# Second layer's routed experts computed on scored token-expert pairs sorted by expert, in four parts, beside a dense shared expert

## The chip, the core and the metric

The kernel is one program on one core of a Trainium2 chip. The metric is the device time of one execution in microseconds (us), lower is better. The core has a matrix engine (TensorE, PE in the rows; its weight loads stand apart as PEld), three engines that work on 128 partitions in parallel (VectorE = DVE, ScalarE = ACT, GpSimd = POOL), and a queue engine (SyncE = SP) that here only starts transfers. Each engine takes its instructions in program order; between engines only semaphores count. POOL starts the indirect transfers (one row address for each of the 128 partitions). Data lie in SBUF (128 partitions), matmul results in PSUM (eight banks of 512 fp32 columns, `ps[:, bank, :]`).

## What is computed

`x` holds 8 sequences of 512 tokens of 128 numbers. Two layers, each `x = x + s * silu(ffn)`, where `s` is a recurrence (layer 0) or a causal linear attention (layer 1), and both read the layer-normalised `x`. The change is in the feed-forward part of layer 1:

```
def _L1_ffn_ref(x, gate_w, w1, w2, w3, w1s, w2s, w3s):   # 8 experts, hidden size 128, TOP_K = 2
    scores = softmax(xt @ gate_w.T)
    top_scores, sel = top_k(scores, TOP_K)
    order = argsort(sel.reshape(-1), stable=True)
    token_idx, eid = order // TOP_K, sel.reshape(-1)[order]
    routed_in = xt[token_idx] * top_scores_sorted[:, None]
    for e in range(NUM_EXPERTS):
        xe = where(eid == e, routed_in, 0)
        h = silu(xe @ w1[e]) * (xe @ w3[e])
        out_routed += where(eid == e, h @ w2[e], 0)
    hs = silu(xt @ w1s[0]) * (xt @ w3s[0])               # the shared expert, all tokens
    out = hs @ w2s[0]
    out = out.at[token_idx].add(out_routed)
```

The score multiplies the input of an expert, not its output. All weights and results are fp32.

## The kernel before

**Layer 0.** Tokens are sorted by group of experts into 35 tiles of 128 rows with 32 indirect scatters (L394), and `late_slot(n)` runs one tile after the other for n = 0 to 34: gate and up as three fp32r products each (L838 to L840: rounded weight and rounded input, rounded weight and rest, rest and rounded), the hidden tile's turn (L868), the down product in fp32 (L858), and an indirect transfer that brings the tile's rows home to DRAM (`bring_home`, L404 on POOL). SP loads them again sequence by sequence into `xnT` (`load_y`, L329): sequences 0 to 2 after the first 16 tiles, 3 to 7 only when tile 34 is home.

**Layer 1** runs sequence after sequence, j = 0 to 7, each in 18 slots u. Slot u is half an expert: `gate_up(j, u)` makes one 512-column product of the gate or up weight of expert u // 2 with all 512 tokens, again as three fp32r products (L956 to L958). DVE multiplies the routed ones by the token's score for this expert, spread over all partitions (`scaled`, L1470; the score is 0 where the expert isn't chosen), ACT takes the silu (L654), POOL multiplies gate and up (`hidden1`, L440), and PE adds `unit_down` (L967, fp32, 512 columns) of all nine experts into one bank. So every token passes every expert. The result has features on partitions, and `turn_result` (L972) turns it back. Score rows go through DRAM: SP stores them and loads them again, spread over 128 partitions (1 MB each, two for a sequence, L338).

Between these slots lie, by numbers written out in the code, the attention of the same sequence (`scores` L913, `turn_keys` L920, `sum_state` L928, `attend` L940 and L942, masks L1434, `attended` L1449) and the preparation of the next two (gated result `gated` L1344 and L1347, statistics `stats1` L1351, `variances` L1357 to L1360, `scales` on POOL L421 and L423, `normalised` L602, turn L888, `values` with the router's columns L895, `query` L900, `key` L903, `relu` and exponentials L620 to L630, router order `ranks` L1380 to L1385, `scored` L1389 to L1394). The ranks say for each token and expert how many experts are ahead of it; rank below 2 is chosen.

## Time and profile before

| | |
|---|---|
| runs | 408.09, 412.56 and 543.4 us, median 412.56 us |
| profiled execution | 414.17 us, of which its span (first to last instruction) 412.3 us |
| mean granted TensorE clock | 0.959 of 2.4 GHz |
| busy | PE 383.7 us (93%), PEld 282.1, DVE 269.9 (65%), ACT 224.7 (54%), POOL 218.6 (53%) |

Share of PE in 40 equal slices of the span, in tenths, and the clock in tenths of full speed:

```profile
PE   7979673799999999899999999999999999999995
PEclk9868777799999999999999999999999999999999
```

Layer 0's slots begin near slice 8 (80 us), layer 1's near slice 18 (181.5 us) and run to the end. Matmuls overlap one another, so what one costs is read as the distance between two starts, not as its own duration.

### The profile page before, as it was taken

The page shows a single profiled execution, that of the slowest core. Times are in us where ns is not written, and L with a number is a line of the kernel's source. Part 1 is how long each engine was busy: PE and PEld are TensorE (multiplying, and loading weights), DVE is VectorE, ACT ScalarE, POOL GpSimd, SP SyncE. Part 2 cuts the span into 40 slices and gives each one's busy share as a digit, 9 for nine tenths or more (in the row PEclk, how much of TensorE's full clock was granted, in tenths as well). Part 3 has the DMA queues.
Part 4 walks back from the last instruction along what each step waited for, and adds up shares of the span by engine and source line. Part 5 has one row for each costly group of instructions (what it writes and reads, how often), then busy time and mean ns, then how long its engine had stood idle before and what let it go on. Part 6 is the DMA issues. An engine that isn't in the chain of part 4 may idle for free.

```text
span 412.3 us, 6279 instructions
## 1 busy us (share of the span) xinstructions
PE 383.7 (93%) x1853; PEld 282.1 (68%) x1853; DVE 269.9 (65%) x755; ACT 224.7 (54%) x447; POOL 218.6 (53%) x214
## 2 busy tenths in 40 slices
PE   7979673799999999899999999999999999999995
PEld 5674321598989888786666767667677667676772
DVE  5988942353434365527959859779689598676563
ACT  3667453454554557768756464493574664742311
POOL 4437876017653344247653936827638549268362
PEclk9868777799999999999999999999999999999999
DMA  8996311601001200006080050140410601503200
GB/s 230 243 345 255 104 52 52 172 4 36 21 25 45 80 27 19 21 33 231 2 293 16 21 212 0 51 181 1 161 72 0 232 1 29 203 0 118 115 25 26
DMA packets 26400, 38.70 MB, mean 94 GB/s; under 512 B 2640, under 2 KB 22608, under 8 KB 23936
## 3 DMA queue, kind: packets, MB, share of 16 engines
q1 hardware_dynamic: 24224, 33.87, 25.2%
q0 software_dynamic: 2144, 4.44, 3.2%
q8 instruction: 16, 0.26, 0.3%
q14 instruction: 16, 0.13, 0.1%
HBM read 29.22 MB, written 9.08 MB: 93 GB/s over the span
## 4 chain that ended last, share of the span: by engine, by line
PE 72%; DVE 10%; ACT 9%; another core or an unknown queue 3%; issue 3%; DMA 1%; POOL 1%; SPq 0%; POOLq 0%; DVEq 0%; ACTq 0%
PE ps L967 10%; PE ps L858 7%; PE ps L958 6%; PE ps L956 6%; PE ps L957 6%; PE ps L779 5%; PE ps L838 4%; PE ps L840 4%; PE ps L839 4%; PE ps L868 4%; PE ps L942 3%; PE ps L895 2%; DVE score L1394 2%; DVE pr L1391 2%
## 5 line engine op out<-in xcount | busy, mean ns | idle before, releaser
L440 POOL TENSOR_TENSOR gu<-gu 128x512 f32<-128x512 f32 x64 | 84.0, 1317 | 86.6 <-DVE gu L1470 81.4
L956 PE MATMUL ps<-xc_round,w_round 128*128 128x512 f32 x144 | 82.8, 575 | 0.6 <-DVE gu L1458 0.5
L654 ACT ACTIVATE gu<-gu 128x512 f32<-128x512 f32 x64 | 40.3, 630 | 75.3 <-DVE gu L1470 75.2
L967 PE MATMUL ps<-gu,w2s 128*128 128x512 f32 x144 | 73.4, 593 | 0.5 <-POOL gu L440 0.5
L404 POOL DMA_INDIRECT home_y<-sorted_sb,home x35 | 34.1, 974 | 70.6 <-ACT sorted_sb L581 46.5
L958 PE MATMUL ps<-xc_round,w_rest 128*128 128x512 f32 x144 | 56.9, 395 | 0.0
L957 PE MATMUL ps<-xc_rest,w_round 128*128 128x512 f32 x144 | 56.5, 393 | 0.0
L1470 DVE TENSOR_TENSOR gu<-ps,w_raw 128x512 f32<-128x512 f32 x64 | 43.8, 687 | 19.0 <-PE ps L958 18.4
L1320 DVE TENSOR_TENSOR sx_rest<-ps,sx_round 128x128 fp32r<-128x128 f32 x35 | 10.2, 291 | 63.4 <-ACT sx_round L567 54.1
L838 PE MATMUL ps<-w_round,sx_round 128*128 x70 | 35.0, 501 | 10.3 <-issue 6.2
L576 ACT COPY h0T<-ps 128x512 f32<-128x512 f32 x35 | 20.6, 587 | 43.5 <-PE ps L868 42.1
L394 POOL DMA_INDIRECT sorted_rows<-sorted_sb,slot x32 | 33.4, 1044 | 15.8 <-issue 9.5
L858 PEld LDWEIGHTS ps<-w0d,h0T 128*128 128x128 f32 x280 | 36.5, 191 | 3.4 <-issue 0.4
L956 PEld LDWEIGHTS ps<-xc_round,w_round 128*128 128x128 f32 x144 | 27.3, 190 | 15.8 <-issue 12.1
L957 PEld LDWEIGHTS ps<-xc_rest,w_round 128*128 128x128 f32 x144 | 27.4, 190 | 14.5 <-issue 12.9
L858 PE MATMUL ps<-w0d,h0T 128*128 x280 | 36.9, 275 | 0.0
L967 PEld LDWEIGHTS ps<-gu,w2s 128*128 128x128 f32 x144 | 26.7, 188 | 8.2 <-POOL gu L440 1.5
L1330 DVE SCALAR_TENSOR_TENSOR h<-sg,sorted_sb,ps 128x256 f32<-128x256 f32 x70 | 30.2, 473 | 3.1 <-PE ps L868 2.6
L958 PEld LDWEIGHTS ps<-xc_round,w_rest 128*128 128x128 f32 x144 | 27.0, 188 | 6.1
L1470 DVE TENSOR_TENSOR gu<-ps,w0d 128x512 f32<-128x512 f32 x32 | 21.7, 688 | 12.4 <-PE ps L958 12.3
L779 PE MATMUL ps<-xnT,a0w 128*128 128x512 f32 x48 | 29.3, 761 | 0.0
L840 PE MATMUL ps<-w_rest,sx_round 128*128 x70 | 28.5, 408 | 0.0
(202 smaller groups left out, 768.5 us busy)
## 6 DMA issues: line engine op xcount, KB each, us to landing
w_raw<-score_rows SPq DMA_DIRECT2D x8, 1024.0 KB, 6.7
sorted_sb<-score_rows SPq DMA_DIRECT2D x4, 1024.0 KB
w0d<-score_rows SPq DMA_DIRECT2D x4, 1024.0 KB, 6.9
sorted_rows<-zero_rows SPq DMA_DIRECT2D x1, 2358.0 KB, 16.5
xa<-in_x SPq DMA_DIRECT2D x8, 256.0 KB, 5.1
w_raw<-in_gate_up SPq DMA_DIRECT2D x1, 2048.0 KB, 13.7
xnT<-home_y SPq DMA_DIRECT2D x8, 256.0 KB, 6.9
out_x<-xa SPq DMA_DIRECT2D x7, 256.0 KB, 2.4
```

The source lines that it names most:

```text
L404: pool.indirect_dma_start(home_y, bass.IndirectOffsetOnAxis(ap=home[:, n:n + 1], axis=0), sorted_sb[:, n, 0:P], None).then_inc(y_home[0 if ...
L440: pool.tensor_tensor(gu[:, e % RING, 1, :], gu[:, e % RING, 0, :], gu[:, e % RING, 1, :], ALU.mult).then_inc(s["m_h"], 1)
L654: nc.scalar.activation(gu[:, e % RING, 0, :], gu[:, e % RING, 0, :], ACT.Silu).then_inc(s["m_sg"], 1)
L779: last = pe.matmul(ps[:, 3 * par + i, :], a0w[:, i * P:(i + 1) * P], xnT[:, q * SEQ:(q + 1) * SEQ], start=True, stop=True)
L838: pe.matmul(bank, sx_round[:, par, :], w0_round[:, c], start=True, stop=False)
L840: return pe.matmul(bank, sx_round[:, par, :], w0_rest[:, c], start=False, stop=True)
L858: last = pe.matmul(ps[:, bank, 0:P], h0T[:, par, c * P:(c + 1) * P], w0d[:, bass.ds(g + c * P, P)], start=(c == 0), stop=(c == HC - 1))
L956: pe.matmul(bank, w13_round[:, c], xc_round[par][:, :], start=True, stop=False)
L957: pe.matmul(bank, w13_round[:, c], xc_rest[par][:, :], start=False, stop=False)
L958: pe.matmul(bank, w13_rest[:, c], xc_round[par][:, :], start=False, stop=True).then_inc(s["m_gu"], 1)
L967: pe.matmul(ps[:, 3, :], w2s[:, w * P:(w + 1) * P], gu[:, e % RING, 1, :], start=(e == 0), stop=(e == E1)).then_inc(s["m_y"], 1)
L1470: nc.vector.tensor_tensor(gu[:, e % RING, part, :], ps[:, BANKS[u % RING], :], spread[j % 2][(e - 1) // (E1 // 2)][:, c:c + SEQ], ALU.mult ...
```

## The change

Layer 1 no longer runs by sequence. `MAIN` is a list of 41 places b = 0 to 40: 6 empty ones, 6 quads of part 0, 6 of part 1, the shared expert of sequences 0 and 1, 6 quads of part 2, 6 of part 3, the shared expert of sequences 2 to 7, 3 empty ones. A part is two sequences: 1024 tokens, 2048 pairs of token and chosen expert, sorted by expert. Each expert's pairs are rounded up to whole tiles of 128, so a part has room for 16 + 7 = 23 tiles, and all 23 are computed; a quad is four of them (three in a part's last). Attention of sequence k is at places 3k, 3k + 1 and 3k + 2.

For a part, DVE ranks and counts (place `ROUTE_AT` = 3, 6, 15 for parts 1 to 3), PE sums the counts over partitions (`place2`), DVE works out the address of each pair, multiplies the normalised rows by their two scores and works out each tile's expert (next place). POOL scatters the rows to DRAM, eight indirect transfers for a sequence; SP loads the part's 23 tiles; after the quads it stores the results, and POOL gathers them, again eight for a sequence. A quad takes plain fp32 matmuls, weights chosen by registers loaded from `expert`. The shared expert stays dense, in fp32 too. The sum over pairs is made on DVE (`summed`). The normalised `xn` now lives in the scatter's source, the first three sequences are prepared in layer 0's slots (`GY_AT`, `TURN_AT`), the ReLU of the feature map moves from ACT to DVE, the products of gate and up from POOL to DVE, and the splitting of the layer-1 weights, the score rows' way through DRAM and the turn of the result fall away.

```diff
-T_GY = (23, 27)
-T_TURN = 27
+PART2 = ((0, 1), (2, 3), (4, 5), (6, 7))
+TILES2 = tuple(TOPK1 * TPS * len(p) + E1 - 1 for p in PART2)
+QUAD = 4
+GY_AT = (20, 23, 27)
+TURN_AT = (24, 27, 33)
+MAIN = (6 * [None] + [("q", 0, i) for i in range(QUADS2[0])] + [("q", 1, i) for i in range(QUADS2[1])]
+        + [("s", k, 0) for k in (0, 1)] + [("q", 2, i) for i in range(QUADS2[2])] + [("q", 3, i) for i in range(QUADS2[3])]
+        + [("s", k, 0) for k in range(2, SEQS)] + 3 * [None])
+ATT_AT = tuple(3 * k for k in range(SEQS))
+GATED_AT = (None, None, None, 1, 2, 3, 8, 9)
+TURNED_AT = (None, None, None, 2, 4, 5, 12, 14)
+LOGITS_AT = (None, None, None, 3, 5, 6, 13, 15)
+ROUTE_AT = (None, 3, 6, 15)
...
+            scatter_pairs(0)
+            scales(3)
+            scatter_pairs(1)
+            scales(4)
+            scales(5)
+            scatter_pairs(2)
+            scatter_pairs(3)
+            scatter_pairs(4)
+            scales(6)
+            scatter_pairs(5)
+            scales(7)
+            gather_pairs(0)
+            gather_pairs(1)
+            scatter_pairs(6)
+            scatter_pairs(7)
+            for k in range(2, SEQS):
+                gather_pairs(k)
...
+            def gather_pairs(k):
+                p = part2_of(k)
+                pool.wait_ge(pairs_stored[p], 32)
+                wait(pool, "c_z", k - GABS + 1)
+                for r in range(TOPK1):
+                    for t in range(TPS):
+                        pool.indirect_dma_start(
+                            gab[k % GABS][:, r, t, :], None, pairs_y[p],
...
+            def unit_gate(m):
+                kind, k, _ = UNITS[m]
+                wait(pe, "m_h", m)
+                if kind == "q":
+                    q = QUAD_UNITS.index(UNITS[m])
+                    pe.wait_ge(s["q_xT"], q + 1)
+                    for t in range(tiles_in(UNITS[m])):
+                        w = pe.snap(at_w13[t], min_val=0, max_val=W13 - 3 * P)
...
+                        last = pe.matmul(ps[:, GATE + t // 2, o:o + 2 * P].rearrange("p (a c) -> p a c", c=P),
...
+            for b, unit in enumerate(MAIN):
+                before = MAIN[b - 1] if b > 0 else None
+                after = MAIN[b + 1] if b + 1 < len(MAIN) else None
+                if unit:
+                    unit_gate(unit_no(unit))
+                if after and after[0] == "q":
+                    experts_of(at_w13, after, 0)
+                for k in range(SEQS):
+                    if b == ATT_AT[k] + 2:
+                        z_free()
+                        sum_state(k)
+                        z_read[0] = ("c_state_out", k + 1)
+                if before:
+                    unit_down(unit_no(before))
+                if unit and unit[0] == "q":
+                    experts_of(at_w2, unit, 1)
+                if after and after[0] == "q":
+                    turn_pairs(QUAD_UNITS.index(after))
+                for k in range(SEQS):
+                    if b == ATT_AT[k] and k > 0:
+                        query(k)
+                        key(k)
+                        z_free()
+                        values(k)
...
+            def rows_of(k):
+                dve.wait_ge(s["c_turned"], k + 1)
+                by = [score2[:, r, TPS * k:TPS * (k + 1)].unsqueeze(2).broadcast_to([P, TPS, P]) for r in range(TOPK1)]
+                link(nc.vector.tensor_tensor(rsrc[k][:, :, 1, :], rsrc[k][:, :, 0, :], by[1], ALU.mult))
+                nc.vector.tensor_tensor(rsrc[k][:, :, 0, :], rsrc[k][:, :, 0, :], by[0], ALU.mult).then_inc(s["c_rows"], 1)
...
+                for p in range(1, PARTS2):
+                    if b == ROUTE_AT[p] + 1:
+                        slots_of_pairs(p)
+                        scored(p)
+                        for k in PART2[p]:
+                            rows_of(k)
+                        experts_of_tiles(p)
```

What TensorE runs in a place. Of before, nine rows from a sequence's slots 4 to 6: two halves of a routed expert (three fp32r rows each, L956 to L958) between two downs (L967) and the state (L928); `m_free` is DVE's scaling, `m_h` POOL's product.

```order
L967 MATMUL ps<-gu,w2s 128x512 [waits m_h]
L956 MATMUL ps<-xc0_round,w13_round 128x512 [waits m_free]
L957 MATMUL ps<-xc0_rest,w13_round 128x512
L958 MATMUL ps<-xc0_round,w13_rest 128x512
L956 MATMUL ps<-xc0_round,w13_round 128x512 [waits m_free]
L957 MATMUL ps<-xc0_rest,w13_round 128x512
L958 MATMUL ps<-xc0_round,w13_rest 128x512
L967 MATMUL ps<-gu,w2s 128x512 [waits m_free,m_gf]
L928 MATMUL ps<-vo,key_rows 128x129 [waits c_keys_out]
```

Of the change, the piece from one place (b = 12) on, behind its gate matmuls: registers with the experts (`TENSOR_LOAD`), the three downs of the quad before (L1029, a weight address in an `ISA` row each), four turns of the next quad's rows (L989), query (L933, waits for the attention result of the sequence before, `c_s1`), key, and the turn of this quad's hidden tiles (L1014), which waits for DVE (`m_h`).

```order
L982 TENSOR_LOAD expert [waits expert_ready]
L1028 ISA [waits q_hT,q_y]
L1029 MATMUL ps<-w2s,hT 128x128
...
L982 TENSOR_LOAD expert [waits expert_ready]
L989 MATMUL ps<-cst,sorted_sb 128x128 [waits q_xT,pairs_in1_0]
L989 MATMUL ps<-cst,sorted_sb 128x128 x3
L933 MATMUL ps<-xnT,a1w 128x512 [waits c_s1,c_xT]
L936 MATMUL ps<-xnT,a1w 128x512
L940 MATMUL ps<-vg_w,xnT 128x128 [waits c_state_out]
L940 MATMUL ps<-vg_w,xnT 128x128 x3
L1014 MATMUL ps<-cst,hq 128x128 [waits q_hT,m_h]
L1014 MATMUL ps<-cst,hq 128x128 x3
```

The three fp32r rows of an expert half over 512 tokens have become four 256-column fp32 rows (L1001) for a quad, and one place holds one unit with what lies around it.

On DVE, the router's work of one sequence in before: nine rows, from one scaling to another. The scalings (L1470) that TensorE's banks wait for stand between all of it.

```order
L1470 TENSOR_TENSOR gu<-ps,sorted_sb 128x512
L1434 TENSOR_TENSOR at<-ps,cst 128x256
L1434 TENSOR_TENSOR at<-ps,cst 128x128
L1470 TENSOR_TENSOR gu<-ps,sorted_sb 128x512
L1389 TENSOR_REDUCE rs<-e1 128x4
L1390 RECIPROCAL rs<-rs 128x4
L1391 TENSOR_TENSOR pr<-e1,rs 128x32
L1394 SCALAR_TENSOR_TENSOR score<-rank,pr 128x4x8
L1470 TENSOR_TENSOR gu<-ps,sorted_sb 128x512
```

Of the change, the end of the same for part 2 (place b = 7, then b = 8): the last rows of a run of 30 between two products of gate and up (L1572). Twelve for the addresses (L1446 to L1459) and seven for the scores (L1478 to L1484) stand right ahead of these.

```order
L1489 TENSOR_TENSOR rows3456<-rows3456,score2 128x4x128
L1490 TENSOR_TENSOR rows3456<-rows3456,score2 128x4x128
L1489 TENSOR_TENSOR rows3456<-rows3456,score2 128x4x128
L1490 TENSOR_TENSOR rows3456<-rows3456,score2 128x4x128
L1463 TENSOR_TENSOR past2<-cst,ends2 1x168
L1466 TENSOR_TENSOR past2<-past2,step2 1x168
L1468 TENSOR_REDUCE expert_f<-past2 1x24
L1469 CAST expert<-expert_f 1x24
L1466 TENSOR_TENSOR past2<-past2,step2 1x168
L1468 TENSOR_REDUCE expert_f<-past2 1x24
L1469 CAST expert<-expert_f 1x24
L1572 TENSOR_TENSOR hq<-sgq,ps 128x512
```

The product of place 8 is the last row, behind the whole of the part's routing.

On POOL, the last rows of the change (sequences 4 to 7; `pairs_y2` holds the results of part 2, and `pairs_stored3` says that part 3's are in DRAM). In before POOL ends with products L440 and one sum L445.

```order
L487 DMA w0d<-pairs_y2,slot2 128x128 [waits c_z,pairs_stored2]
L487 DMA w0d<-pairs_y2,slot2 128x128 x7
L487 DMA w0d<-pairs_y2,slot2 128x128 [waits c_z,pairs_stored2]
L487 DMA w0d<-pairs_y2,slot2 128x128 x7
L487 DMA sorted_sb<-pairs_y3,slot2 128x128 [waits c_z,pairs_stored3]
L487 DMA sorted_sb<-pairs_y3,slot2 128x128 x7
L487 DMA sorted_sb<-pairs_y3,slot2 128x128 [waits c_z,pairs_stored3]
L487 DMA sorted_sb<-pairs_y3,slot2 128x128 x7
```

The last sixteen gathers stand behind the store of the last quads.

## Rows read from the trace of the kernel before

**Rows 1.** Windows: us, busy of PE, PEld, DVE, ACT, POOL, clock, DMA share, GB/s.

```profile
181.50:209.70 28.20, 27.05 (x138) 20.19 (x139) 19.83 (x52) 20.65 (x36) 18.51 (x16) 1.00 0.32 115
294.40:322.60 28.20, 28.01 (x125) 19.65 (x124) 22.65 (x54) 16.03 (x28) 16.64 (x14) 1.00 0.23 85
```

**Rows 2.** Groups by line: engine, tile, shape, count, busy us, mean ns, idle before.

```profile
L956 PE MATMUL ps<-xc_round,w_round 128*128 128x512 f32 x144 | 82.8, 575 | 0.6 <-DVE gu L1458 0.5
L967 PE MATMUL ps<-gu,w2s 128*128 128x512 f32 x144 | 73.4, 593 | 0.5 <-POOL gu L440 0.5
```

**Rows 3.** Timeline of PE in a sequence: start, us, line, tile, count.

```profile
301.17 1.02 PE L967 MATMUL ps<-gu,w2s 128*128 128x512 f32 x2
...
302.26 0.40 PE L957 MATMUL ps<-xc_rest,w_round 128*128 128x512 f32 x1
302.49 0.39 PE L958 MATMUL ps<-xc_round,w_rest 128*128 128x512 f32 x1
...
310.48 0.60 PE L972 MATMUL ps<-cst,gf 128*128 128x128 f32 x4
```

**Rows 4.** Timeline of POOL: indirect scatters and transfers home.

```profile
31.09 0.96 POOL L394 DMA_INDIRECT sorted_rows<-sorted_sb,slot  x1 [0.30 <-issue]
32.35 0.95 POOL L394 DMA_INDIRECT sorted_rows<-sorted_sb,slot  x1 [0.30 <-issue]
...
46.31 2.02 POOL L394 DMA_INDIRECT sorted_rows<-sorted_sb,slot  x1 [0.30 <-issue]
...
129.44 0.96 POOL L404 DMA_INDIRECT home_y<-sorted_sb,home  x1 [1.88 <-ACT sorted_sb L581]
...
177.44 1.04 POOL L421 TENSOR_TENSOR rstd<-var,minus_half 128x4 f32<-128x4 f32 x1
...
187.74 0.96 POOL L404 DMA_INDIRECT home_y<-sorted_sb,home  x1 [0.30 <-issue]
```

**Rows 5.** Timeline of SP's queue: the first loads of what came home.

```profile
131.72 1.46 SPq L329 DMA_DIRECT2D xnT<-home_y  x3
```

**Rows 6.** Page, part 6: transfers, KB each, median us from issue to landing.

```profile
xnT<-home_y SPq DMA_DIRECT2D x8, 256.0 KB, 6.9
out_x<-xa SPq DMA_DIRECT2D x7, 256.0 KB, 2.4
```

**Rows 7.** Timeline of DVE.

```profile
147.85 0.69 DVE L1344 TENSOR_TENSOR gy<-gy,sT 128x512 f32<-128x512 f32 x1
148.58 0.69 DVE L1347 SCALAR_TENSOR_TENSOR xa<-gy,xa 128x512 f32<-128x512 f32 x1
149.30 0.87 DVE L1351 BATCH_NORM_STATS2 st<-xa 128x6 f32<-128x128 f32 x4
...
176.03 0.22 DVE L1394 SCALAR_TENSOR_TENSOR score<-rank,pr 128x32 f32<-128x32 f32 x1
...
302.14 0.42 DVE L1380 TENSOR_TENSOR ahead<-lg 128x256 f32<-128x256 f32 x1
```

**Rows 8.** Groups of DVE, shapes apart.

```profile
L1449 DVE SCALAR_TENSOR_TENSOR s<-ps,den,bo 128x128 f32<-128x128 f32 x32 | 9.6, 341 | 0.0
L1237 DVE TENSOR_TENSOR past<-cst,steps 1x286 f32<-1x286 f32 x1 | 0.4, 437 | 0.0
```

**Rows 9.** Timeline of ACT: exponential, change of table, silu.

```profile
302.07 1.04 ACT L630 ACTIVATE tg<-tg 128x1024 f32<-128x1024 f32 x1
303.13 1.28 ACT L654 ACT_TABLE_LOAD   x1
304.42 0.63 ACT L654 ACTIVATE gu<-gu 128x512 f32<-128x512 f32 x1
```

**Rows 10.** Windows around TensorE's wait at the start of layer 0's slots.

```profile
64.00:68.00 4.00, 1.45 (x4) 0.38 (x2) 0.00 (x0) 2.15 (x4) 3.08 (x4) 0.97 0.20 67
68.00:72.00 4.00, 0.37 (x1) 0.38 (x2) 0.72 (x4) 1.15 (x3) 2.40 (x3) 0.50 0.15 50
```

More of the change, by code:

```diff
@@ L368, in _ @@
+            load_pairs(3)
+            store_pairs(2)
+            store_pairs(3)
+            for j in range(2, SEQS):
+                store_out(j)
+            sp.wait_ge(o_stored, 16 * SEQS)
         @block.gpsimd
@@ new lines, in logits, with place2, query @@
+                last.then_inc(s["c_logits"], 1)
+            def place2(p, bank):
+                n = TPS * len(PART2[p])
+                pe.wait_ge(s["counted2"], p + 1)
+                pe.matmul(ps[:, bank, 0:E1], lower, cum2[:, :, n - 1], start=True, stop=True)
+                pe.matmul(ps[:, bank, E1:2 * E1], ones, cum2[:, :, n - 1], start=True, stop=True).then_inc(s["placed2"], 1)
+            def query(k):
+                pe.wait_ge(s["c_xT"], k + 1)
+                wait(pe, "c_s1", k)
+                pe.matmul(ps[:, BX, :], a1w[:, 0:P], xnT_of(k), start=True, stop=True).then_inc(s["c_q"], 1)
@@ L1089, in _, with z_free @@
-            unit_down(SEQS - 1, E1 - 1)
-            unit_down(SEQS - 1, E1)
-            for i in range(2):
-                pe.wait_ge(s["m_gf"], SEQS + i)
-                turn_result(SEQS - 1, slice(2 * i, 2 * i + 2), (4, 6)[i])
+            pe.wait_ge(s["f_xr"], SORTED)
+            values(0)
+            pe.wait_ge(s["f_y"], SORTED - 1)
+            key(0)
+            pe.wait_ge(s["f_y"], SORTED)
+            pe.wait_ge(s["f_h"], SORTED)
+            z_read = [("c_vo", 1)]
+            def z_free():
+                pe.wait_ge(s[z_read[0][0]], z_read[0][1])
@@ new lines, in attended, with unit_hidden @@
+                last.then_inc(s["c_s1"], 1)
+            def unit_hidden(m):
+                kind, k, _ = UNITS[m]
+                n = tiles_in(UNITS[m])
+                dve.wait_ge(s["m_sg"], m + 1)
+                if kind == "q":
+                    ups = ps[:, GATE:GATE + 2, :].rearrange("p b c -> p (b c)").rearrange("p (t c) -> p t c", c=2 * P)[:, 0:n, P:2 * P]
+                else:
+                    ups = ps[:, GATE + 1, :].rearrange("p (t c) -> p t c", c=P)
+                quads = sum(u[0] == "q" for u in UNITS[:m])
+                wait(dve, "q_hturned", quads)
+                if m > 0 and UNITS[m - 1][0] == "s":
+                    dve.wait_ge(s["m_down"], m)
+                nc.vector.tensor_tensor(hq[:, 0:n, :], sgq[:, 0:n, :], ups, ALU.mult).then_inc(s["m_h"], 1)
```

1102 lines of the change are left out of this document (537 added, 565 removed).

## Prediction

> **What bounds the kernel now.** First the windows, one for each sequence of layer 1 [rows 1]: PE is busy 28.01 of 28.2 us, DVE 22.65, POOL 16.64, ACT 16.03, at a clock of 1.00. The sequences follow each other at this distance to the end, so in layer 1 (181.5 to 412.3 us, 230.8 us) TensorE is the bound and no other engine waits for anything but it. What it does there, the groups say [rows 2]: 144 triples that begin with L956, and 144 halves (72 matmuls) of L967. Their price is the distance between starts in the timeline [rows 3]: fp32r with 512 columns 0.23 us (302.26 to 302.49), a triple 0.69; the two halves of the fp32 down from 301.17 to 302.03 (one such step before 302.26), 0.86. Four turns cost about 0.44 (0.60 with the overlap). I take 0.21 us for an fp32 matmul of 128 columns and 0.43 for 256, a quarter and a half of 0.86.
>
> **What TensorE saves.** Of a sequence's 28.2 us, 18 triples take 12.4, nine downs 7.7, the result's turn 0.44; 7.6 stay for attention and preparation. Removed are 16 triples (11.0), 8 downs (6.9) and the turn: 18.4. The shared expert goes from 2 x 0.69 + 0.86 to three times 0.86, 0.3 more. Added are 11.5 tiles a sequence (23 for two): a turn 0.11, gate and up 0.43, a turn of the hidden tile 0.11, down 0.21, so 0.86 a tile or 3.45 a quad, 9.9 a sequence. TensorE saves 18.4 - 0.3 - 9.9 = 8.2 us a sequence, 65 in all, and needs some 165 of the 230.8. If it stayed the bound, the kernel would take 347 us. It doesn't: everything it now works on passes DVE, POOL and DRAM first, with few tiles ahead. I walk through these.
>
> **The opening, to the end of place 6.** Until here layer 0 is as before, its added work (one sequence more prepared, ranks of 8 tiles) hidden under slots of 2.8 us; the last tile goes home at about 186 instead of 187.74 [rows 4], since three triples no longer stand ahead of its down. From there:
> - POOL: a scatter comes every 1.26 us (31.09 to 32.35), eight for a sequence, 10.1 us, so sequence 0 ends at 197. Scales: 1.04 + 0.2 = 1.3. Sequence 1: 198.6 to 208.7. What POOL sends lands 1.3 us after it (transfer at 129.44 to 130.4, loads at 131.72 [rows 4, 5]); a load of 512 KB by the 6.9 us in a queue of several and the 2.4 of a single one of 256 KB [rows 6] I put at 3.5. First pairs at 213.5.
> - DVE, which is later still. Sequence 3 can only be loaded at 188, is gated and normalised by 200.3, turned at 201.3. TensorE has waited 4 us then, and goes at half clock, as in the row of 0.50 after a wait [rows 10]. Query, key and values, 2.6 us at full clock, take it to 206.5; values out 0.7, router columns 0.6: 207.9.
> - Ranks for 8 tiles: a linked 512-column operation starts every 0.73 us (147.85 to 148.58 [rows 7]), three are 2.2; five short ones of 0.22 and a gap of 0.04 (176.03) make 1.3: 3.5 us, to 211.6. Behind them on DVE stand two features (1.2), and gating and statistics of sequence 5 (1.44 + 1.5, by 0.87 for the first of three steps), to 215.7, then masks 1.2.
> - The routing block: 19 short operations 4.9, four row products 2.9, seven for the tiles' experts 2.2 (168 elements on one partition: between 0.22 and the 0.44 of 286 [rows 8]). 10.0 us, to 227. Then `attended`, four of 0.34 [rows 8] and three short, 1.7: 228.6. Only then may the query of place 6 start (`c_s1`), although the first quad's gate is done at 221.
> - Place 6: again a wait of 6 us ahead, so 4.7 us for query, key, values; out and router columns 1.5; ranks 3.5, and `place2` waits for them: 238.5.
>
> So the first 52 us hold about 22 us of TensorE's work.
>
> **Places 7 to 23.** With attention in every third place a place has 3.45 + 7.6/3 = 6.0 us of TensorE's work (5.8 where no sequence is prepared). ACT needs less: 4 copies or silus of 0.6 and, once in three places, 1.04 + 2 x 1.28 for exponential and tables [rows 9] and two ReLUs, some 4.3 a place; it costs the place after an exponential 0.5. 17 x 5.9 = 100.3. Added: the ranks of part 3 in place 15, waited for like those above, 4.6; the routing blocks of parts 2 and 3 in places 7 and 16. The product of the next quad (L1572) stands behind the block, the hidden turn behind that: masks end about where the place ends, so the turn of places 8 and 17 comes at 10.0 + 0.7 + 0.4 = 11.1 instead of 5.6: 5.5 us each, 11. For half clock after these three waits [rows 10] I add 5. Place 23 ends at 238.5 + 100.3 + 4.6 + 11 + 5 = 359.4.
>
> **Places 24 to 31**, quads alone. Gate 1.71; 0.2 until ACT sees it, silu 0.6, product 0.69, 0.1, turn 0.44 make 3.75, and the copies of the turned rows behind the result's copy 3.9, against 3.45 of PE: 8 x 3.9 = 31.2, to 390.6.
>
> **The tail.** The last results are copied out 3.1 us into place 32, their store of 704 KB takes 4 (one of 256 KB 2.4 [rows 6]). Only now do the gathers of sequences 6 and 7 start, 16 on POOL. No gather stands in the trace: the nearest row is a scatter, 1.26 with the gap; its bounds are 0.95 (no gap) and 2.32 (the row at 46.31 and the gap). I take 1.26, as it too writes 128 row addresses: 20.2, bounds 15 and 37. Landing 1.5, two sums, silu and two products 3.6, store 2.4, end 0.8. Sum 35.6 us, of which TensorE's last six shared experts (6 x 2.6) hide 15 but shorten nothing. Span 426 us. The profiled execution of before has 414.17 for a span of 412.3, and its median is 412.56, so I put the time at **426 us**, 3% over before.
>
> What hides the rest: the zeroing of the pairs' buffers (6.3 MB) delays the first tiles home, but their rows are first wanted 16 tiles on; POOL's scatters for parts 1 to 3 end 20 us and more ahead of their quads; the splitting of weights (POOL) and score rows (SP) were hidden before and give nothing.
>
> **A rule against the change.** The rows show a clock of 1.00 in layer 1 before, and 0.50 after TensorE had stood still [rows 1, 10]. The Trainium skill, "TensorE: Matmul & The Clock Gate", section "HAM oscillation — how this bites in real kernels", says that waits for transfers between bursts of matmuls send the clock back to half and that each burst pays again. By it the places after the waits are dear; if the clock stayed full, the same sum would be 4 + 5 us less, about 415.
>
> **Rivals.**
> - *The walk, slower* (426; own range 421 to 441): chance 0.56, of which 0.14 for its upper part: DVE holds up POOL. The scatter at 46.31 took 2.02 instead of 0.96 us while DVE worked on SBUF [rows 4]; if every second transfer on the path (32 of them) and the registers' loads on PE (48, not seen in before as a gap) cost that much, 15 us more, 441. The Trainium skill, "GPSIMD Engine Reference", section "1. Specifications", says that POOL shares its SBUF interfaces with VectorE and meets two-input instructions there; that row agrees.
> - *DVE's blocks are shorter, within 2%* (about 412): full clock (9 less) and short operations at 0.2 instead of 0.26 (3 us over three blocks), or landing and loads faster by 2. Chance 0.30.
> - *POOL alone sets the opening, faster* (about 392): if DVE's work in places 3 to 6 fits under POOL's chain, the first gate is at 217 and place 6 ends at 223 rather than 238.5, and if the two later blocks fit in their places too (5.5 each, and clock 5), 426 - 15.5 - 11 - 5 = 394. It decides when a block takes under 5 us. For it: before, DVE's share was below TensorE's. Against: these operations are chained one by one, and the product stands behind them. Chance 0.14.
> - *It computes no less than before.* 92 tiles for 64 tiles' worth of pairs are fixed by the room for rounding; this is in the sum.
>
> **Numbers.** About 2% is what a measurement here can tell from no change. Faster by more than 2% (under 404) 0.14, within 2% (404 to 421) 0.30, slower 0.56. The range that leaves 2 in 10 out reaches from 401 (half of the third rival) to 441: the likeliest case's own range begins at 421.
>
> **What would show it.** PE idle ahead of query L933 in place 6 and ahead of the hidden turn L1014 in places 8 and 17, 4 to 6 us each, released by DVE; clock near 0.5 right after; quads alone every 3.9 us; the last sixteen gathers 1.26 us apart with PE idle beside them. I am wrong if PE in the 17 mixed places is busy over 90%, if a gather costs far from 1.26, or if the block is under 7 us.

## The result, and the profile after

The changed kernel took **524.33 us** (median of 3, 520.13 to 527.39) beside 412.56 before: a ratio of **1.277, 95% interval 1.250 to 1.304**. The forecast was 426 us, range 401 to 441. The direction was right, and the size was not: 3% was forecast, 28% came.

Much of that turned out to depend on the chip. On another chip the same kernel took **448.75 us** beside 398.83 before, **1.129 (1.120 to 1.137)**. So there are two misses: about 37 us in the kernel's own work (448.75 beside 412, see below), and 75 us more on the first chip. In what follows "first chip" is that of the first result, and "a quiet chip" is one where the kernel before takes 396 to 402 us. (On the first chip one execution of before took 543.4 us; no trace shows why.)

Page of after, parts 1, 3 and 4: busy us, share and instructions of each engine; two DMA queues; the chain that ended last.

```profile
PE 371.2 (71%) x1965; PEld 298.8 (57%) x1965; DVE 239.5 (46%) x735; ACT 221.8 (42%) x439; POOL 229.3 (44%) x244
...
q1 hardware_dynamic: 51600, 35.31, 23.1%
q0 software_dynamic: 6240, 12.84, 8.1%
...
PE 42%; another core or an unknown queue 17%; ACT 12%; DVE 12%; issue 8%; POOL 5%; DMA 2%; SPq 1%; POOLq 0%; DVEq 0%; ACTq 0%
```

No engine is the bound: 71% of PE, 46% of DVE. A quarter of the chain (17% and 8%) is on no engine at all. The windows that answer [rows 1], and two more (us, busy of PE, PEld, DVE, ACT, POOL, clock, DMA share, GB/s):

```profile
181.50:209.70 28.20, 19.20 (x119) 16.20 (x118) 15.65 (x48) 14.28 (x29) 21.56 (x12) 0.94 0.14 44
294.40:322.60 28.20, 21.43 (x132) 18.33 (x130) 9.91 (x28) 15.70 (x29) 11.73 (x13) 0.94 0.37 105
380.00:420.00 40.00, 13.38 (x68) 10.93 (x67) 8.11 (x13) 7.27 (x11) 23.00 (x24) 0.70 0.22 62
420.00:460.00 40.00, 37.30 (x239) 31.86 (x238) 13.21 (x30) 24.12 (x41) 4.48 (x5) 1.00 0.32 89
```

Where before had 28.01 of 28.2 us of PE, after has 21.43; from 380 to 420 us it is 13.38 of 40, with POOL the busiest engine. In the 40 us behind that POOL is nearly silent and PE is back at 37.30. That contrast is the main clue. Timeline of after in the bad stretch (start, us, instruction, idle time before it and its releaser):

```profile
392.91 0.95 POOL L487 DMA_INDIRECT sorted_sb<-pairs_y,slot  x1 [0.31 <-issue]
393.78 0.59 ACT L684 COPY xT<-ps 128x512 f32<-128x512 f32 x1 [9.29 <-remote]
...
394.61 3.47 PE L1001 MATMUL ps<-w13s,xT 128*128 x8 [8.74 <-issue]
...
402.88 0.56 DVE L1544 TENSOR_TENSOR at<-ps,mask 128x384 f32<-128x384 f32 x1 [12.60 <-issue]
...
412.67 0.56 DVE L1544 TENSOR_TENSOR at<-ps,mask 128x384 f32<-128x384 f32 x1 [9.24 <-remote]
...
414.78 0.37 ACT L674 COPY key_rows<-ps 128x256 f32<-128x256 f32 x1 [19.89 <-remote]
```

Each of these ACT and DVE instructions waits for a result of TensorE. The matmuls that they wait for are recorded long before: the last of them, the turn of the keys (L954), at 385.49. The profile names no instruction that ends these waits ("remote", "issue"). Beside them POOL issues indirect transfers every 1.26 us, the last at 409.20. I call such a wait a **hold**. On the quiet chip (a_again, below) the same instructions stand like this, and no ACT, DVE or PE instruction behind 110 us has an unexplained wait over 1.8 us:

```profile
347.56 0.58 ACT L684 COPY xT<-ps 128x512 f32<-128x512 f32 x1
349.75 0.63 ACT L710 ACTIVATE zf<-zf 128x512 f32<-128x512 f32 x1 [1.61 <-DVE zf L1581]
350.28 0.35 ACT L674 COPY key_rows<-ps 128x256 f32<-128x256 f32 x1
```

### The profile page after: what moved, and what is told of

Its sections match the earlier page's. It is cut to its first block, busy times and chain, and to the rows that moved or that the text cites. A ratio compares the mean times of both kernels' runs of the same rounds, so it can differ in the third digit from the quotient of the medians.

```text
span 525.6 us, 6617 instructions
## 1 busy us (share of the span) xinstructions
PE 371.2 (71%) x1965; PEld 298.8 (57%) x1965; DVE 239.5 (46%) x735; ACT 221.8 (42%) x439; POOL 229.3 (44%) x244
## 4 chain that ended last, share of the span: by engine, by line
PE 42%; another core or an unknown queue 17%; ACT 12%; DVE 12%; issue 8%; POOL 5%; DMA 2%; SPq 1%; POOLq 0%; DVEq 0%; ACTq 0%
PE ps L1001 6%; PE ps L884 5%; PE ps L805 4%; POOL sorted_sb L487 3%; PE ps L864 3%; PE ps L894 2%; PE ps L866 2%; PE ps L865 2%; PE ps L1029 2%; POOL e L468 2%; PE ps L920 2%; ACT sorted_sb L536 1%; PE ps L1007 1%; ACT sgq L694 1%
## 5 line engine op out<-in xcount | busy, mean ns | idle before, releaser
L477 POOL DMA_INDIRECT pairs_x<-rows,slot x40 | 40.6, 1014 | 64.5 <-DVE rows L1490 53.0
L1001 PE MATMUL ps<-w13s,xT 128*128 x184 | 53.2, 440 | 18.8 <-ACT xT L684 9.7
L1572 DVE TENSOR_TENSOR hq<-sgq,ps 128x512 f32<-128x512 f32 (+1 forms) x32 | 21.4, 670 | 88.4 <-ACT sgq L694 63.0
L487 POOL DMA_INDIRECT w0d<-pairs_y,slot x32 | 30.4, 951 | 66.6 <-DMA pairs_y<-xs_even 57.5
L1001 PEld LDWEIGHTS ps<-w13s,xT 128*128 128x128 f32 x184 | 39.2, 225 | 26.3 <-issue 20.6
L487 POOL DMA_INDIRECT sorted_sb<-pairs_y,slot x32 | 32.6, 1017 | 29.6 <-DVE zf L1581 20.2
L1029 PEld LDWEIGHTS ps<-w2s,hT 128*128 128x128 f32 x184 | 26.2, 210 | 9.9 <-issue 8.9
L1029 PE MATMUL ps<-w2s,hT 128*128 x184 | 27.2, 294 | 6.0 <-ACT hT L699 4.0
L865 PE MATMUL ps<-w_round,sx_rest 128*128 x70 | 29.1, 416 | 0.0
L612 ACT ACTIVATE sg<-ps 128x512 f32<-128x512 f32 x35 | 21.0, 599 | 17.8 <-PE ps L866 11.3
L1014 PE MATMUL ps<-cst,hq 128*128 128x128 f32 x92 | 16.7, 308 | 13.7 <-DVE hq L1572 12.3
```

Source lines behind the costliest of these rows:

```text
L477: pool.indirect_dma_start(pairs_x[p], bass.IndirectOffsetOnAxis(ap=slot2[:, r, TPS * k + t:TPS * k + t + 1], axis=0), rsrc[k][:, t, r, :], ...
L487: pool.indirect_dma_start(gab[k % GABS][:, r, t, :], None, pairs_y[p], bass.IndirectOffsetOnAxis(ap=slot2[:, r, TPS * k + t:TPS * k + t + ...
L865: pe.matmul(bank, sx_rest[:, par, :], w0_round[:, c], start=False, stop=False)
L1001: last = pe.matmul(ps[:, GATE + t // 2, o:o + 2 * P].rearrange("p (a c) -> p a c", c=P), xT[:, q % 2, t * P:(t + 1) * P], w13s[:, bass.ds( ...
L1029: last = pe.matmul(ps[:, DOWN, t * P:(t + 1) * P], hT[:, t * P:(t + 1) * P], w2s[:, bass.ds(w, P)], start=True, stop=True)
```

## Experiments

### The holds by themselves

A small program (not the model) sets stretches one after another: TensorE and ScalarE hand a bank to and fro 28 times, or TensorE runs 450 matmuls in one go, beside different work of POOL and SP.

```diff
+SECTIONS = (("pa", None), ("pa", "scatter"), ("pa", "gather"), ("pa", "pool"), ("pa", "plain"),
+            ("mm", None), ("mm", "scatter"), ("mm", "gather"), ("da", None), ("da", "scatter"), ("da", "gather"), ...)
+for t in range(STEPS):                       # "pa", on PE: wait for ACT's copy t, then
+    for c in range(4): pe.matmul(ps[:, t % 2, c * P:(c + 1) * P], cst[:, 0:P], xa[:, c, :], ...)
```

(Shortened: "pa" is the to and fro of TensorE and ScalarE, "mm" the 450 matmuls, "da" VectorE with ScalarE; the second word is what runs beside it.)

> Not the model: a small program of 13 stretches that times the disputed cost by itself; its output is a copy of x. In a stretch TensorE and ScalarE hand a PSUM bank to and fro 28 times (four 128x128 fp32 matmuls, one copy), or VectorE and ScalarE do, or TensorE runs 450 matmuls in one go, and beside it stands nothing, or 36 scatters, 36 gathers, POOL products, or plain transfers of SP's queue. The profile of the changed kernel shows instructions that wait for a TensorE result and go on 2 to 20 us after its last recorded matmul, always while POOL issues indirect transfers 1.26 us apart. Theory (indirect transfers hold TensorE's results up): the to and fro takes about 28 x 1.7 = 48 us alone, beside POOL products and beside plain transfers, and 10 to 40 us more beside 36 gathers or scatters (45 us of them); the 450 matmuls lengthen by a like amount only if TensorE itself is held. VectorE with ScalarE is not lengthened. Rival (the stalls come of TensorE's register loads or of its instruction stream and the transfers only stand beside them by chance): gathers change nothing in the stretches without register loads, under 2 us each.

First copy to last: 74.3 us alone (48 were expected), 74.3 beside POOL products, 74.3 beside plain transfers, but 101.2 beside 36 scatters and 103.6 beside 36 gathers. The 450 matmuls took 102 us alone, 141 beside scatters, 135 beside gathers (POOL's transfers began at 566.73 and 707.66, the next stretch at 842.80). VectorE with ScalarE: 30.0 alone, 33.8 and 33.9 beside transfers, with no hold. With four register loads ahead of each step it was 87.7 alone and 107.0 beside gathers. ScalarE's copies beside the scatters, which ran from 99.72 to 145.14:

```profile
109.99 0.59 ACT L136 COPY cop<-ps 128x512 f32<-128x512 f32 x1 [2.17 <-issue]
112.75 0.59 ACT L136 COPY cop<-ps 128x512 f32<-128x512 f32 x1 [2.17 <-PE ps L160]
116.80 0.59 ACT L136 COPY cop<-ps 128x512 f32<-128x512 f32 x1 [3.47 <-PE ps L160]
125.27 0.59 ACT L136 COPY cop<-ps 128x512 f32<-128x512 f32 x1 [7.88 <-remote]
140.73 0.59 ACT L136 COPY cop<-ps 128x512 f32<-128x512 f32 x1 [14.87 <-remote]
150.57 0.59 ACT L136 COPY cop<-ps 128x512 f32<-128x512 f32 x1 [9.26 <-remote]
153.33 0.59 ACT L136 COPY cop<-ps 128x512 f32<-128x512 f32 x1 [2.17 <-PE ps L160]
```

The to and fro keeps its pace beside the first dozen transfers, is then held for 8, 15 and 9 us, and is free again 5 us after the last. In the 450 matmuls nothing waits for a result, and there TensorE's own starts are drawn apart (each matmul leaves two rows; scatters from 566.73):

```profile
610.47 0.37 PE L164 MATMUL ps<-cst,xa 128*128 128x128 f32 x1 [2.43 <-issue]
613.27 0.37 PE L164 MATMUL ps<-cst,xa 128*128 128x128 f32 x1 [2.43 <-issue]
616.78 0.37 PE L164 MATMUL ps<-cst,xa 128*128 128x128 f32 x1 [3.14 <-issue]
617.49 89.81 PE L164 MATMUL ps<-cst,xa 128*128 128x128 f32 x787 [0.34 <-issue]
```

From 576.7 to 617.5 it starts 30 of the 900 rows, up to 3.5 us apart, and then at once one every 0.11 us, as alone. So the holds are TensorE's, matmuls as well as what waits for them; they come beside indirect transfers in either direction, and they need nothing else of this kernel. The rival falls as far as it says register loads or chance: without register loads all four stretches beside such transfers are held. What the transfers act on isn't shown. One more rival is untested: every execution listed here has a granted clock on record, so each was recorded by the profiler, and TensorE leaves by far the most rows (900 in 102 us, as many weight loads, and VectorE with ScalarE only 56 in 30); whether TensorE is also held when nothing is recorded is open.

The same program then went on with other forms of the transfers: twelve, spaced, in bursts, fewer rows, each waited for, plain ones from POOL.

> The small program again (TensorE and ScalarE to and fro, 28 times, 77 us alone, 2.75 us each), now with other forms of the transfers beside it: 36 gathers back to back; 12 of them; 36 each followed by two POOL products (about 2.6 us apart) or by one (about 1.9 us); bursts of six with about 8 us of products between; 36 with 32 of the 128 rows; 36 that each wait for the landing of the one before; 36 plain ones issued by POOL; and 450 matmuls in one go beside 36 spaced ones. Theory A (POOL's transfers are issued faster than something behind them takes them, and TensorE is held while the backlog stands; in the first small program the holds began 13 to 14 us after the first of 36 in three stretches of three): 12 gathers cost under 2 us, spaced ones and bursts cost under 3 us each, back to back 25 to 30 us; those that wait for landing nothing. Theory B (each gather takes TensorE some 0.8 us wherever it stands): 12 cost about 10 us, the spaced ones 25 to 30 us like the others. The quarter rows tell whether rows or instructions count: under 3 us if rows.

There all nine stretches of the to and fro, "36 back to back" among them, were 74.3 us. The kernel before took 397.93 us on that chip, for 407.61 on the chip of the first small program. That made the chip itself a suspect:

> The small program with the eight forms of transfers beside TensorE and ScalarE, and two more stretches of 450 matmuls in one go, alone and beside 36 gathers back to back. On the chip of the first small program 36 transfers back to back cost TensorE 27 to 29 us in the to and fro; on the chip of the second nothing at all (74.3 us in each form). Theory (a property of the chip on which it runs, not of the program): it comes out as one of the two, all or nothing, and together with the kernel before on the same chip: holds where that takes 406 us and more, none where it takes 398 to 400. If there are holds: twelve gathers and those that wait for landing cost under 2 us, 36 back to back 25 to 30. Rival (the first program's scatters left something behind): no holds on either kind of chip, since this program has no scatter.

Again 74.3 us for each form, and 450 matmuls beside 36 gathers took 100.7 us for 102.6 alone:

```profile
776.61 102.62 PE L169 MATMUL ps<-cst,xa 128*128 128x128 f32 x900 [0.16 <-issue]
879.64 100.74 PE L169 MATMUL ps<-cst,xa 128*128 128x128 f32 x900 [0.41 <-DVEq L187]
```

The program without a scatter doesn't explain it either: m5_spacing has 36 scatters in a stretch of its own.

> The small program with two more forms: scatters, and gathers of which every eighth is waited for until it has landed. Theory (holds belong to the chip): with before at 397 to 400 us no stretch is over 75 us. On a chip with holds (before over 405): 36 back to back cost 25 to 30 us, as 36 scatters do; with a wait for landing after each eight, or 2.6 us apart, under 3 us (theory A, a backlog), or 15 us and more (theory B, each transfer).

74.3 us in all ten, the scatters' included, and m4_spacing and m6_spacing (the same forms once more) gave the same. Holds were seen on the first chip and on that of m1_side_by_side (which may be the same); none on three others, in five runs of the small program. Beside those five the kernel before took 397.9 to 399.7 us (medians; the last two share most of its executions), on the first two 412.6 and 407.6. The forms were thus never measured where there are holds; whether it is a property of the chip or of something that ran there at that time isn't settled either.

### The holds in the kernel

> The changed kernel with all 128 indirect transfers of the second layer (64 scatters, 64 gathers) replaced by plain ones of the same bytes on SP's queue, so the rows are not sorted and the result is another; all other work stands. Theory (indirect transfers hold up TensorE's results, beside POOL's own 1.26 us each): no wait for a TensorE result over 2 us that goes on after its last matmul is left behind 215 us, the second layer loses 17 to 25 per cent of the span and the time is about 400 to 430. Rival (only POOL's own time on the path goes, 20 us in the opening and 20 in the tail; the stalls of 5 to 20 us stay): 475 to 490.

```diff
-                        pool.indirect_dma_start(pairs_x[p], ..slot2.., rsrc[k][:, t, r, :], None)
+                sp.dma_start(px_t[p][:, 8 * (k % 2):8 * (k % 2) + 8, :], rsrc[k].rearrange("p t r d -> p (t r) d"))
-                        pool.indirect_dma_start(gab[k % GABS][:, r, t, :], None, pairs_y[p], ..slot2..)
+                sp.dma_start(gab[k % GABS].rearrange("p r t d -> p (r t) d"), py_t[p][:, 0:TOPK1 * TPS, :])
```

(Shortened; the rows go unsorted, one plain transfer for eight indirect ones.) 453.45 us beside 407.61: 1.116 (1.105 to 1.127). The kernel before scattered from 405.6 to 423.2 us on this chip, so each ratio found there (this one and those of a_more_gathers and a_exp_on_act) is on record as unclear; the 87 us to a_exp_on_act's 540.54 on the same chip are clear without it. It ran on a chip with holds; its last is at 114.08 us, beside the homes of layer 0's tiles, which are still indirect:

```profile
114.08 0.58 ACT L633 COPY h0T<-ps 128x512 f32<-128x512 f32 x1 [8.57 <-remote]
```

Nothing is held behind it, which is what the theory said of the trace. The time lies between the theory's range (400 to 430) and the rival's (475 to 490), 23 us over the one and 22 under the other: the theory's range left out the kernel's own 37 us, and the gate of place 6 comes at 248.5 us, 11 later than in nearly the same form on a quiet chip (a_plain_exp, below, 237.5), with the holds of layer 0 left in.

> The changed kernel with 24 more gathers on POOL behind those of sequence 3 (about 410 to 440 us), where POOL is idle and places run in 3.9 to 6 us each now; their rows go to a place nobody reads. Theory (indirect transfers hold up TensorE's results): the stretch gets stalls of 3 to 10 us and the time grows by 10 to 25 us. Rival (stalls are not tied to POOL's transfers): POOL ends them before part 2 is stored, nothing waits, under 3 us.

```diff
+            for i in range(3):
+                for t in range(2 * TPS):
+                    pool.indirect_dma_start(rows3456[:, i, t // 2, t % 2, :], None, pairs_y[0], ..slot2[:, 0, t]..)
```

559.06 us, 1.374 (1.362 to 1.385) on the chip of a_plain_all. The changed kernel itself has no run on this chip, so the cost of 24 transfers that nobody waits for, 30 us of POOL's time, is read twice: 19 us over a_exp_on_act (540.54, this chip) and 35 over the first result (524.33). From the gate of place 6 to that of place 32, where they lie, it is 269.4 us for 240.9 and 235.8: 28 and 34 more, beyond the 10 to 25 expected. ScalarE in the stretch:

```profile
420.02 0.37 ACT L681 COPY key_rows<-ps 128x256 f32<-128x256 f32 x1 [25.55 <-remote]
441.72 0.60 ACT L701 ACTIVATE sgq<-ps 128x512 f32<-128x512 f32 x1 [21.33 <-remote]
```

And the changed kernel on a quiet chip:

> The changed kernel as it stands, once more, on the chip of the small program beside it. Theory (TensorE is held beside POOL's transfers on some chips only): with holds 520 to 535 and 1.28 to 1.31 of before; without them the time is that of the work itself: the same kernel without indirect transfers, 440 to 450, and 5 to 15 us for the tail's gathers and for POOL's queue, so about 450 to 460 or 1.13 to 1.15 of before, and no hold over 2 us in the trace. Rival (the second small program only missed them, the real kernel always has them): 520 to 540 on either chip.

448.75 us, as expected without holds. Its stages against after's, by the starts of the gates L1001 and L1007: the gate of place 6 comes at 236.8 for 249.4; from there to the gate of place 24 it is 136.5 us for 189.7, places 24 to 31 take 32.2 for 46.0, the rest 40.4 for 40.4. All of it lies where POOL's transfers run beside TensorE's work.

> The changed kernel with its 64 scatters as they are and only the 64 gathers of the second layer replaced by plain transfers on SP's queue (the result is another). By the traces of the changed kernel the holds of TensorE behind 250 us that lie beside gathers sum to about 50 us (326 to 338, 386 to 415, 458 to 476) and the tail pays 16 gathers, 20 us, less what plain ones take. Theory (both kinds of transfer hold TensorE alike): 524 to about 470, and 450 is reached only when the scatters go as well, 15 to 25 us. Rival (only scatters hold it, gathers merely wait): 505 to 510.

440.08 us, 1.108 (1.100 to 1.117), on a quiet chip. It can't speak on holds there. Against a_again (1.129) it gives the gathers' own price without holds, 8 us by the ratios; 7.0 of it show in the tail (33.4 us for 40.4 from the gate of place 32 to the end). The scatters that it keeps cost nothing that can be measured (a_plain_exp without them, on the same chip, takes 443.78).

> The changed kernel, POOL's wait for the zeroing put late as in a_zero_late (1.107 of before without holds), and POOL waits for the landing of each sequence's eight scatters or gathers before the next. On a chip without holds: 1 to 2 us for each of 16 waits, nearly all off the path, so 1.11 to 1.12 of before. On a chip with holds, where the changed kernel takes 1.28 to 1.31: by theory A (a backlog behind the transfers) about 1.15, by theory B 1.26 and more.

448.59 us, 1.125 (1.117 to 1.134), on a quiet chip. Beside a_zero_late, which it contains, the sixteen waits cost 7 us, a little more than I put (1.11 to 1.12); the question it was made for stays open.

### The kernel's own 37 us

POOL's power for the exponentials of part 0 takes 10.58 us where 128x4 take 1.04 [rows 4], and I had not costed it.

```profile
169.49 10.58 POOL L468 TENSOR_TENSOR e<-euler,lg 128x64 f32<-128x64 f32 x1
```

> The changed kernel with the exponentials of part 0 made by ScalarE's Exp behind slot 30 in place of POOL's power (10.58 us at 182.7 us). Theory (the power delays the last tiles' way home and the scores of part 0, and with them the whole opening, about 204 us for 186): 10 to 15 us less, 524 to about 511. Rival (the opening is set by VectorE's chain, the power is hidden): under 4 us.

```diff
-                if n == LG_AT:
-                    powers(0)
+                if n == LG_AT + 1:
+                    router_exp(0)          # on ScalarE
```

540.54 us, 1.316 (1.298 to 1.335), not faster. Its trace has a hold of 16.78 us at 64.86, in the scatters of layer 0 that it shares with before, so the comparison said little. Twice more, without holds:

> The changed kernel with part 0's exponentials by ScalarE in place of POOL's power of 10.58 us, beside the changed kernel on the same chip. The theory of the power (it holds up the last tiles' way home and VectorE's scores): 8 to 12 us under the changed kernel. Rival, which the two runs without indirect transfers speak for (1.116 of before with the power, 1.115 without): VectorE's routing chain ahead of it ends no earlier, under 3 us.

> The changed kernel without indirect transfers in the second layer (plain ones of the same bytes on SP's queue, rows unsorted, so another result), and with the exponentials of part 0 by ScalarE instead of POOL's power of 10.58 us. Against the same kernel with the power (450 to 453 us). Theory (the power holds the way home of the last tiles and VectorE's scores, and so the opening): 8 to 12 us less, about 442. Rival (VectorE's routing chain between slots 30 and 35 sets the opening alone): under 3 us less.

1.124 (1.118 to 1.130) beside 1.129 for a_again on the same chip, and 1.115 (1.108 to 1.123) beside 1.116 for a_plain_all on another. Neither has the 8 to 12 us of the theory, so the rival holds: the power is hidden. VectorE waits 0.86 us for it (at 191.90 in a_plain_all's trace), and the homes that pile up behind it are sent 1.3 us apart until the last tile is computed anyway. The power is dear and costs nothing here.

What does cost is the row of slots. From the silu of slot 20 to that of slot 34 it is 46.5 us before and 60.9 in a_again. POOL, ACT and PE of a_again:

```profile
120.17 0.96 POOL L454 DMA_INDIRECT home_y<-sorted_sb,home  x1 [0.30 <-ACT sorted_sb L621]
...
126.30 0.63 ACT L636 ACTIVATE gy<-xnT 128x512 f32<-128x512 f32 x1 [3.61 <-DMA xnT<-home_y]
...
140.15 0.66 PE L914 MATMUL ps<-cst,tg 128*128 128x128 f32 x4 [1.75 <-ACT tg L648]
145.07 1.04 PE L920 MATMUL ps<-vg_w,xnT 128*128 128x8 f32 x8 [1.43 <-ACT xnT L654]
...
171.49 0.39 PE L927 MATMUL ps<-cum,cst 128*128 128x8 f32 x2 [1.83 <-DVE cum L1438]
```

A prepared sequence takes 0.66 + 1.04 us of PE and makes it wait 1.75 and 1.43 us, 4.9 together; there are now three of them and one totals step. The first row is the tail of a backlog: POOL waits for the zeroing before its first tile goes home.

> The changed kernel; POOL waits for the zeroing of the pairs' buffers (6.3 MB on SP's queue from 75 to about 90 us) only ahead of the first scatter of pairs instead of ahead of the first tile's way home. In the changed kernel the homes then run back to back until 124 us, the silu of sequence 0 waits 3.6 us for its rows at 126.3, and slot 20 takes 7.0 us instead of 2.8. Theory (this backlog stretches the slots): 3 to 5 us less than the changed kernel, 1.129 to about 1.118 of before on a chip without holds. Rival (the slots behind take it up): under 1 us.

```diff
-            pool.wait_ge(s["zeroed2"], 16 * PARTS2)
             for n in range(SORTED):
...
+            pool.wait_ge(s["zeroed2"], 16 * PARTS2)
             scatter_pairs(0)
```

443.12 us, **1.107 (1.100 to 1.114)**, some 8 us less than a_again by the ratios where 3 to 5 were expected, the fastest form found with the right sorting; it is still 10.7% over before. The silu of sequence 0 now follows without a wait:

```profile
119.64 0.27 ACT L621 COPY sorted_sb<-ps 128x128 f32<-128x128 f32 x1
119.80 0.65 ACT L636 ACTIVATE gy<-xnT 128x512 f32<-128x512 f32 x1
```

Slot 20 takes 3.3 us instead of 7.0, and slots 20 to 34 54.1 instead of 60.9. The remaining 7.6 us over before would be paid by two more prepared sequences of 4.9, less what is hidden; that share was read from the rows, not tried.

> The changed kernel; of the routing blocks of parts 2 and 3 on VectorE (9.2 us in one piece) the scores, the row products and the tiles' experts (about 6 us) stand behind the hidden product of the next place instead of ahead of it. In the changed kernel TensorE's hidden turn waits 3.5 us at place 8 and 4.3 at place 17 for that product. Theory (the place of the block costs what the forecast says, 5.5 us each less what is hidden): both waits go, 5 to 8 us less, 1.129 to about 1.112 of before on a chip without holds. Rival (the block moves the wait to the attention behind it, query of places 9 and 18): under 2 us less.

```diff
+                for p in range(2, PARTS2):
+                    if b == ROUTE_AT[p] + 2:      # behind unit_hidden of that place
+                        scored(p); rows_of(k) for its sequences; experts_of_tiles(p)
```

1.123 (1.119 to 1.126), 2 us less by the ratios, which can't be told from nothing: the rival's outcome (under 2). The wait ahead of the hidden turn of place 8 is gone, and a longer one stands ahead of the query of place 9. a_again:

```profile
265.24 0.98 PE L1014 MATMUL ps<-cst,hq 128*128 128x128 f32 x4 [3.52 <-DVE hq L1572]
```

and a_block_split:

```profile
269.42 2.04 PE L933 MATMUL ps<-xnT,a1w 128*128 128x512 f32 x2 [5.34 <-DVE sT L1556]
```

At the other block it is the same: 4.29 us ahead of the hidden turn of place 17 become 3.44 ahead of the query of place 18. Where VectorE's block of 9 us stands only chooses who waits.

## Why the prediction was wrong, and where it was right

The fair comparison for the sum is a_again: the sum was made on a trace that had holds of its own beside layer 0's scatters, and before is 13.7 us shorter on the quiet chip, so it says 412 there, and 448.75 was measured. (That all 13.7 us lie ahead of layer 1 is taken, not shown: no trace of before from a quiet chip is kept.) Windows of a_again, cut at the last tile's result, the query of place 6, the gate of place 24 and the shared expert behind place 31:

```profile
189.70:239.60 49.90, 32.06 (x131) 25.62 (x129) 29.19 (x99) 20.65 (x36) 26.70 (x29) 0.62 0.29 86
239.60:373.30 133.70, 110.73 (x671) 93.02 (x670) 72.01 (x194) 74.02 (x122) 75.14 (x79) 0.92 0.35 98
373.30:405.50 32.20, 29.45 (x181) 24.59 (x180) 6.54 (x13) 17.10 (x31) 14.03 (x15) 1.00 0.35 98
405.50:445.90 40.40, 18.05 (x80) 11.01 (x78) 20.26 (x30) 8.32 (x14) 19.32 (x19) 0.84 0.33 88
```

- **"Until here layer 0 is as before, its added work hidden under slots of 2.8 us": failed**, the largest step within the kernel. The last tile was to go home at 186, or 172.3 without the holds of before; POOL sends it at 190.68 (the copy it waits for starts at 189.66), 18.4 us late: 14.3 in the slots 20 to 34 (6.7 of them gone with the backlog behind the zeroing) and 4 outside them, not traced further. The sentence "the zeroing delays the first tiles home, but their rows are first wanted 16 tiles on" is the same mistake: the backlog lasted until 125 us, and the rows were wanted at 122.7.
- **The opening from there to the query of place 6**: 42.6 forecast, 48.9 measured, at a clock of 0.62 in the first window. VectorE ends most of TensorE's waits in it, as forecast (4.44 us ahead of the query of place 3, 3.64 ahead of the counts' sums, L927, for part 1). But the wait forecast ahead of the query of place 6 isn't there: VectorE's answer for it is there at 237.8, and the query starts at 239.60 right behind the gate and the turns of its place. There TensorE itself, at half clock through place 5 and this gate, was the later one. The parts were right: scatters 1.26 us apart, ranks 3.2 to 3.5 us (3.5), routing block 9.2 (10.0); what lies between them was put too short.
- **Places 6 to 23**: 130.8 forecast, 133.7 measured. The waits behind the two blocks were 3.5 and 4.3 us for 5.5 each (as a sign, 4 to 6 were named), released by DVE at the turn L1014 as named; so their total came out near although the other work in these places took some 6 us more than put. PE is busy 83% there, under the 90% at which I would have been wrong.
- **Places 24 to 31**: 31.2 forecast, 32.2 measured; the quads are 3.8 to 4.5 us apart for 3.9.
- **Tail**: 35.6 forecast, 40.4 measured. The sixteen gathers took 414.56 to 436.40, 21.8 us for 20.2; a gather takes 0.95 and 0.30 as taken from the scatter, some here up to 1.46. They began later than put, since sequence 6's may only start when its buffer is free (`c_z`): POOL waited 6.41 us there for DVE.
- The rest, 2.9 us, is no step of the kernel: 1.8 around the span of 445.9, which the sum left out, and 1.1 between this execution and the median.

These make 18.4 + 6.3 + 2.9 + 1.0 + 4.8 + 2.9 = 36.3 of the 37 us. The quads and the gathers came out near for the reasons given; places 6 to 23 did so partly by luck, since two errors offset each other. The first two steps are two thirds of the miss.

**The 75 us more on the first chip are a cost put at nothing.** The sum lets POOL's transfers cost POOL's own time alone ("POOL's scatters for parts 1 to 3 end 20 us and more ahead of their quads", in what hides the rest), and TensorE runs beside them as if they weren't there. On the first chip it doesn't: 12.7 us more up to the gate of place 6, 53.2 from there to place 24, 13.8 to place 32 (after beside a_again, whose profiled executions are 79.7 us apart). Why is open. The rows were there. [Rows 10] show TensorE at 1.45 and 0.37 of 4 us beside POOL's scatters of [rows 4], and I read them as a matter of the clock. In that stretch the kernel before has waits ended by nothing known, for instance at the first gate:

```profile
71.63 0.79 PE L838 MATMUL ps<-w_round,sx_round 128*128 x1 [6.18 <-issue]
```

and beside its 35 tiles home, most of them 2.8 us apart, none over 1.8 us. The change put 128 more indirect transfers into the program, in runs of up to 32 at 1.26 us. The rival closest to it, "DVE holds up POOL", has the direction the wrong way round: POOL's transfers took 0.95 to 1.02 us in the mean in layer 1, for 0.97 and 1.04 before, and it was TensorE that stood.

**The rule of the Trainium skill** ("TensorE: Matmul & The Clock Gate", "HAM oscillation — how this bites in real kernels"), that each burst behind a wait pays again: the opening's 0.62 agrees, and 0.92 and 1.00 in the mixed and the last places say that it matters mostly there. I had put 9 us on it; the opening's excess of 6.3 us may partly be its, no run separates them. The Trainium skill, "GPSIMD Engine Reference", "1. Specifications", has POOL share its SBUF interfaces with VectorE. I had weighed that as a loss of up to 15 us: the mean indirect transfer at 1.0 us shows almost none of it.

**The rivals**: "within 2%" and "POOL alone sets the opening" (named 392, summed to 394) both fell on each chip. "Slower" had the larger chance and came, but on each chip by more than its own range, 441 at most.

## What to carry to other kernels

In a row of dependent slots an operation's duration is only part of what it costs: the three prepared sequences had 1.7 us of TensorE's work each and, by the rows, took 4.9, because each step waited for another engine's answer within the same slot. When work is added "under" a stage, add its round trips and not its busy time. Replacing dense work by sorted work trades the busiest engine for a chain over all of them; here the 65 us that TensorE was to save came back as openings, blocks and a tail, with the engine idle 20% of the span (a_again). And before adding many of a kind of transfer, look at the one stretch of the old trace that is full of them, wait by wait: a wait there that ends in no known way may come back with each of them.

## What the runs showed of the hardware

- On one or two chips, beside indirect transfers that POOL issues 1.26 us apart, TensorE's results come 2 to 25 us late and its matmuls start up to 3.5 us apart, mostly from the eighth to fifteenth transfer on until 5 to 9 us behind the last: 27 to 39 us more beside 36 of them, 19 with register loads (m1_side_by_side, a_more_gathers). Beside plain transfers by SP's queue and POOL's arithmetic they do not, and VectorE with ScalarE is not held. On three other chips nothing of the kind was seen. What is behind it stays open, and so does whether it happens when no profile is taken.
- Between the first chip and a quiet one this kernel's time differs by 17% (524 and 449), the kernel before's by 3% (412.6 and 398.8), so a ratio found on one chip need not hold on the next.
- POOL's power takes 10.58 us for 128x64 and 1.04 for 128x4, so about 0.16 us for each element of a partition (an estimate from these two); ScalarE's exponential of 128x64 took 0.26 us, and 1.28 for each of the two table changes around it (a_exp_again).
- An indirect gather of 128 rows of 512 bytes takes POOL 0.95 to 1.02 us in the mean and 0.30 until the next, as a scatter does (1.02).
